# Attention in pairs of steps: one stretch of full-width matmuls, one of 32-column products

## The reference

```
x = x + attention(layernorm(x))
x = x + ffn(layernorm(x))          # base linear + top-2 of 8 rank-16 LoRA experts

attention: q, k, v = x@Wq.T, x@Wk.T, x@Wv.T    split into 16 heads of 32
           q, k = rope(q), rope(k)
           scores = q k^T / sqrt(32), causal mask
           ctx = softmax(scores) v;  out = ctx @ Wo.T
```

## Time and profile before

| | |
|---|---|
| median of 3 runs | 1838.37 us (1838.18 to 1847.95) |
| the profiled execution's own time, its span | 1836.8 us |
| PE busy | 1737.2 us, 95%, 9952 matmuls |
| DVE, POOL, ACT busy | 1167.2, 804.4, 784.3 us |
| granted TensorE clock, mean | 0.965 |

### The profile page before, as it was taken

The page is one execution under the profiler, slowest core; times in us unless marked ns, Lnnn a source line. Parts: engine busy times, 40 slices in busy tenths (PEclk is TensorE's granted clock), DMA queues, the critical chain, the costliest instruction groups (busy, mean ns, idle before and its releaser), DMA issues. The chain is left out here.

```text
span 1836.8 us, 33962 instructions
## 1 busy us (share of the span) xinstructions
PE 1737.2 (95%) x9952; PEld 1010.7 (55%) x9952; DVE 1167.2 (64%) x2630; ACT 784.3 (43%) x1544; POOL 804.4 (44%) x434
## 2 busy tenths in 40 slices
PE   6999995789999999989999998999999996999998
PEld 5888884444444444444445444444444433677776
DVE  6667663687767767657767775776776704566564
ACT  3222221135555545545555554554555563222321
POOL 1333333335655646535655564564664672111211
PEclk9999998599999989989999998999999997999999
DMA  5556545830161161142115006116102003131221
GB/s 172 201 197 220 194 166 174 185 72 24 25 139 25 25 131 33 25 90 70 30 35 124 25 10 137 25 25 135 29 25 71 12 7 101 41 134 69 83 100 47
DMA packets 103259, 157.60 MB, mean 86 GB/s; under 512 B 10544, under 2 KB 43824, under 8 KB 100400
## 3 DMA queue, kind: packets, MB, share of 16 engines
q1 hardware_dynamic: 93296, 136.10, 27.4%
q10 hardware_dynamic: 9792, 19.40, 2.9%
HBM read 96.23 MB, written 58.72 MB: 84 GB/s over the span
## 5 line engine op out<-in xcount | busy, mean ns | idle before, releaser
L771 ACT ACTIVATE a_probs<-a_st 128x512 f32<-128x512 f32 (+3 forms) x1280 | 613.2, 536 | 543.3 <-PE a_st L661 277.7
L618 POOL TENSOR_TENSOR a_pair<-a_probs 128x1024 f32<-128x1024 f32 (+2 forms) x320 | 614.8, 1938 | 396.7 <-ACT a_probs L771 396.7
L790 DVE TENSOR_REDUCE a_part<-a_mx 128x1 f32<-128x512 f32 x768 | 507.7, 684 | 208.8 <-PE a_mx L649 206.8
L649 PE MATMUL a_mx<-a_k_stack,a_q_stack 96*128 96x512 f32 (+3 forms) x1280 | 493.5, 428 | 45.1 <-DMA a_q_stack<-qk_scratch 24.5
L661 PE MATMUL a_st<-a_q_stack,a_k_stack 98*128 98x512 f32 (+3 forms) x1280 | 447.9, 393 | 5.1 <-ACT a_probs L771 2.2
L649 PEld LDWEIGHTS a_mx<-a_k_stack,a_q_stack 96*128 96x128 f32 x1280 | 229.7, 196 | 389.5 <-DVE a_part L790 179.5
L794 DVE CUSTOM_DVE_ANT_0 a_mx<-a_mx,a_mask 128x384 f32<-128x384 f32 (+3 forms) x512 | 250.5, 498 | 140.7 <-PE a_mx L649 138.1
L661 PEld LDWEIGHTS a_st<-a_q_stack,a_k_stack 98*128 98x128 f32 x1280 | 242.8, 193 | 83.6 <-ACT a_probs L771 52.7
L217 POOL TENSOR_TENSOR p_rot<-p_mul 128x1024 f32<-128x1024 f32 x32 | 90.7, 2836 | 213.3 <-DVE p_mul L412 213.3
L675 PE MATMUL a_av<-a_probs,shared 128*32 128x512 f32 (+3 forms) x1280 | 161.7, 551 | 0.7
L675 PE MATMUL a_av<-a_probs,a_v 128*32 128x512 f32 (+3 forms) x1280 | 160.0, 546 | 0.7
(11 more groups left out here) (138 smaller groups left out, 1656.8 us busy)
## 6 DMA issues: line engine op xcount, KB each, us to landing
a_q_stack<-qk_scratch SPq DMA_DIRECT2D x96, 256.0 KB, 4.9
a_k_stack<-qk_scratch SPq DMA_DIRECT2D x21, 1024.0 KB, 13.7
qk_scratch<-p_rot_hi SPq DMA_DIRECT2D x32, 512.0 KB, 3.1
qk_scratch<-p_rot_lo SPq DMA_DIRECT2D x32, 512.0 KB, 3.9
v_scratch<-p_v_st SPq DMA_DIRECT2D x32, 256.0 KB, 6.1
ctx_scratch<-a_ctx_st SPq DMA_DIRECT2D x32, 256.0 KB, 2.4
f_ctx<-ctx_scratch SPq DMA_DIRECT2D x8, 1024.0 KB, 8.9
f_x<-in_x SPq DMA_DIRECT2D x8, 1024.0 KB, 7.8
```

What stands on the lines that cost most here:

```text
L618: pool.tensor_tensor(pair[:, p % 2, h:h + 2, q0:TT], probs[:, s % RING, h:h + 2, q0:TT], probs[:, (s + 1) % RING, h:h + 2, q0:TT], ALU.add ...
L649: pe.matmul(mx_ps[k % BANKS][:, 0:width], q_stack[0:96, t, h, qi * P:(qi + 1) * P], k_stack[par][0:96, h, c * TT:c * TT + width], start=Tr ...
L771: act.activation(probs[:, s % RING, h, q0:TT], st_ps[:, (HG * s + h) % BANKS, q0:TT], ACT.Exp, scale=SCORE_SCALE).then_inc(exp_done, 1)
L790: dve.tensor_reduce(out, mx_ps[k % BANKS][:, :], AX.X, ALU.max).then_inc(max_done, 1)
```

## The change

LAG goes; the ring of probabilities has 4 steps, not 5. PE's `group` now goes by pairs. For pair p it first issues the eight scores of both steps of pair p+1, with the pair's items spread among them, and then `values_and_sums`: the values of both steps of pair p and then their sums, all 32-column products, in one stretch. The wait for the probabilities stands once before it, at the last head of the second step; the waits for the copied values, the turned sums and POOL's two adds stand inside. The semaphore `step_done` becomes `values_done`, one count per pair. ACT, DVE, POOL and SP loop over pairs as well. ACT may write pair p when pair p−2 is done, as POOL may. DVE turns a finished unit's sums at the beginning of the next pair, inverts them after that pair's first item and turns them back after its second. SP stores two pairs after the unit's end and loads queries at the end of the pair that issues a unit's last scores. `plan_items` spreads the same 160 items over 20 pairs (5 to 10 in each), and the first group takes up to 14 in a pair, where it took 7 in a step. The number of matmuls, exps, reductions, adds and DMAs stays.

```diff
-LAG = 2
-RING = 5
+RING = 4
+LAST_PAIR = [e // 2 for e in UNIT_END]
...
-PER_FIRST = 7
+PER_FIRST = 14
...
-    room = [width(s + 1) + width(s) + width(s - LAG) * ((s - LAG) % 2) + 1.0 for s in range(NSTEP)]
-    for e in UNIT_END:
-        room[(e + LAG) % NSTEP] -= 0.8
-        room[(e + LAG + 1) % NSTEP] -= 0.5
+    room = [width(2 * p + 2) + width(2 * p + 3) + 2 * width(2 * p) + width(2 * p + 1) + 0.5 for p in range(NPAIR)]
+    for e in LAST_PAIR:
+        room[(e + 1) % NPAIR] -= 1.0
...
+            def values_and_sums(g, par, p):
+                steps = (2 * p, 2 * p + 1)
+                t, j = STEPS[steps[0]]
+                unit_first, unit_last = j == 0, p in LAST_PAIR
+                q0, q1 = (max(0, STEPS[s][1] - t * SUB) * P for s in steps)
+                pe.wait_ge(exp_done, exps(g, steps[1], HG - 1))
+                if unit_first:
                     pe.wait_ge(av_copied, 4 * g + t + START)
+                for n, (s, q) in enumerate(zip(steps, (q0, q1))):
+                    for h in range(HG):
+                        mm = pe.matmul(av_ps[h * DK:(h + 1) * DK, q:TT], vb[par][:, j + n, h * DK:(h + 1) * DK],
+                                       probs[:, s % RING, h, q:TT], start=unit_first and n == 0,
+                                       stop=unit_last and n == 1, tile_position=(0, h * DK))
+                mm.then_inc(values_done, 1)
+                if unit_first:
+                    pe.wait_ge(sum_turned, 4 * g + t + START)
...
+                pe.wait_ge(pair_added, 2 * (NPAIR * g + p) + 2)
                 for h in range(HG):
...
             def group(g, par, use, next_use, first, last):
+                for p in range(NPAIR):
+                    items = [(n, k) for n, k in items_of_pair(p, first) if not (n and last)]
                     issued = 0
+                    for i in range(2 * HG):
+                        while issued < len(items) and issued * 2 * HG <= i * len(items):
                             n, k = items[issued]
                             item(g + n, (par + n) % 2, next_use if n else use, k)
                             issued += 1
+                        s, h = 2 * p + 2 + i // HG, i % HG
+                        if s < NSTEP:
+                            scores(g, par, s, h)
                         elif not last:
+                            scores(g + 1, 1 - par, s - NSTEP, h)
+                    for n, k in items[issued:]:
+                        item(g + n, (par + n) % 2, next_use if n else use, k)
+                    values_and_sums(g, par, p)
...
             def group(g, first):
+                for p in range(NPAIR):
+                    act.wait_ge(pair_done, pairs(g, p - 2))
+                    for s in (2 * p, 2 * p + 1):
...
             def group(g, first, last):
+                for p in range(NPAIR):
+                    items = [(n, k) for n, k in items_of_pair(p, first) if not (n and last)]
+                    ended = [(g - before, t) for before, t in unit_ended_before(p, 1) if not (before and first)]
+                    for unit in ended:
+                        turn_sums(*unit)
+                    for i, (n, k) in enumerate(items):
+                        item_max(g + n, k)
+                        for unit in ended:
+                            if i == 0:
+                                invert(*unit)
+                            if i == 1:
+                                turn_back(*unit)
...
+                    for n, t in units_ended_at_pair(p, first):
                         if not (n and last):
+                            issued = items_before(p + 1, first)
                             unit_max(g + n, t, NITEM * g + (min(issued, NITEM) if last else issued))
```

More of the change, by code:

```diff
@@ L619, in add_pairs @@
                                            probs[:, (s + 1) % RING, h:h + 2, q0:TT], ALU.add).then_inc(pair_added, 1)
-                    for ahead, t_out in unit_ended_before(s, 1):
-                        if not (ahead and first):
-                            divide(g - ahead, t_out)
+                    for before, t_out in unit_ended_before(p, 1):
+                        if not (before and first):
+                            divide(g - before, t_out)
             def divide(g, t):
@@ L680, in sums @@
[L680 to L699, removed]
+            def values_and_sums(g, par, p):
[5 more added lines that the diff above has]
+                if unit_first:
+                    pe.wait_ge(av_copied, 4 * g + t + START)
+                for n, (s, q) in enumerate(zip(steps, (q0, q1))):
[6 more added lines that the diff above has]
+                    pe.wait_ge(sum_turned, 4 * g + t + START)
+                if q1 > q0:
+                    for h in range(HG):
+                        pe.matmul(sum_ps[h * DK:(h + 1) * DK, q0:q1], ones[:, :], probs[:, steps[0] % RING, h, q0:q1],
+                                  start=unit_first, stop=False, tile_position=(0, h * DK))
+                pe.wait_ge(pair_added, 2 * (NPAIR * g + p) + 2)
+                for h in range(HG):
+                    mm = pe.matmul(sum_ps[h * DK:(h + 1) * DK, q1:TT], ones[:, :], pair[:, p % 2, h, q1:TT],
+                                   start=unit_first and q1 == q0, stop=unit_last, tile_position=(0, h * DK))
@@ L747, in _ @@
             pe.wait_ge(ones_done, 1)
-            for h in range(HG):
-                scores(0, 0, 0, h)
+            for s in range(2):
+                for h in range(HG):
+                    scores(0, 0, s, h)
             pe.wait_ge(first_values, 2 * 16)
@@ L858, in _ @@
             group(GROUPS - 1, False, True)
-            for part_of, _, _ in PARTS:
-                part_of(GROUPS - 1, QT - 1)
+            turn_sums(GROUPS - 1, QT - 1)
+            invert(GROUPS - 1, QT - 1)
+            turn_back(GROUPS - 1, QT - 1)
 class Early:
```

119 lines of the change are left out of this document (35 added, 84 removed).

## The result

The changed kernel takes 1867.33 us (median of 4, 1862.81 to 1876.22), the kernel before 1841.57 in the runs beside it: ratio 1.015, 95% interval 1.0112 to 1.0188. It is slower, as forecast. It lies 17 us above the forecast 1850, inside the stated range (1785 to 1890) and just outside the 1835 to 1865 that was given for the likeliest case. The loss is 26 us, where 12 were forecast. The profiled execution has a span of 1861.1 us at a mean granted clock of 0.94.

The account below looks back on a forecast made before the run. PE sets attention's pace. Per group 48.9 + 84.7 + 1.0 = 134.6, + 6.6 collision + 3.0 clock = 144.2 against 143.0; six times +7, first and last groups −1 + 3 + 1, unit rows +2: span 1849, runs 1850 us, range 1785 to 1890.

Parts of the forecast that it names:

- The collision: At units' maxima, DVE's CAST and subtraction wait for POOL's adds, delaying pairs 2, 12, 10 and 16: +6.6 us per group.
- The clock: Behind PE's waits in pairs 2 and 12, half clock for 3.4 us: 1.5 us each, +3.0 per group.
- Rival 3: Slow clock for long: 10 us at half speed behind each of 16 waits, 5 us each, 1905 us; chance 0.10.
- V: PE's stretch of 32-column products (values and sums) in each pair: 48.9 us per group, 2.81 at two full steps.
- F: PE's stretch of eight scores and n maxima in each pair, by the largest of three chains: 84.7 us per group.
- rival 1: No collision: POOL and DVE stay out of step at units' maxima, 134.6 us per group, 1783 in all; chance 0.24.
- One visit costs 0.28: Each PE visit to 32-column products costs 0.28 us beside its products; 60 become 20 per group, −11.3 us.
- 14.1 us of waits in place of 12.2: Per group, PE's waits for DVE and ACT after the change, against waits and exposed loads before it.
- the ends' −1 and +1: Outside the middle groups: first group −1 us; one step more of scores ahead at the start +1 us.
- 2: Rival: collision, but the clock stays; 141.2 us per group, about 1828 us in all; chance 0.16.
- 5: Rival: visits cost nothing when merged, the 0.28 reappears inside V; +11 us per group, about 1935 us; chance 0.02.
- Rival 4: Full stretches paced by DVE worse than the chain: 0.3 us more in each of 12 full pairs, 1875 us; chance 0.10.

Follow-up runs that it names:

- e1: Changed kernel with a unit's maximum on DVE done by four reductions instead of one reduction, a CAST and a subtraction: 1783.15 us, ratio 0.9675 to before.
- e4: Changed kernel with the third score of pairs 2 and 12 issued 15 times into its bank instead of once: 1843.63 us.
- e6: Kernel before with the unit's maximum by four reductions and DVE reading only 128 columns of each maximum's bank: 1824.0 us, ratio 0.9912.
- e5: Changed kernel with the unit's maximum by four reductions and DVE reading only 128 columns of each maximum's bank: 1705.74 us, ratio 0.9274.

## Why the prediction was right, and where it was not

*The collision: right, in place and mechanism.* It stands at all four units, as laid out: subtractions of 2.26 to 2.32 us for units 0, 1 and 2, a CAST of 1.41 for unit 3. The forecast time line for pairs 11 and 12 holds to some tenths: the CAST was to issue 1.2 us after the adds' start and did so after 1.56, and the subtraction was to end 4.7 after it (8.5 − 3.8) and ended after 4.72. Its size was off. Counted from the first full tile of a pair to that of the next, pair 2 takes 13.4 us and pair 12 12.8 (medians of groups 1 to 6, slow clock included), against 8.25 and 7.63 in e1: 5.2 each, where 2.5 and 2.6, with 1.5 of clock each, were forecast. Pair 10 lost 0.3 and pair 16 1.0, for 0.4 and 1.1. Per undisturbed group collision and clock together cost 147.5 − 136.0 = 11.5 us, against 6.6 + 3.0 = 9.6; with e4's price for the clock, the collision's part is 8.1 for 6.6.

*The clock: right in its price, with luck in its length.* 1.5 for each wait and 3.0 per group were forecast, and e4 gives 1.7 and 3.4. But the forecast reckoned 3.4 us at the lower level, and the windows above show 6.8. By the same reckoning (half of the stretch) that would have been 3.4 us for each wait; e4 puts it at half of this, and why so much of it costs nothing isn't shown. A direct view of the cost is the stretch of values and sums behind the wait of 611.97, which runs from 616.13 to 620.55, 4.42 us:

```profile
616.13 3.63 PE L672 MATMUL a_av<-a_probs,a_v 128*32 128x512 f32 x16
619.55 1.07 PE L684 MATMUL a_sum<-a_pair,a_ones 128*32 128x512 f32 x8
620.55 0.38 PE L643 MATMUL a_mx<-a_k_stack,a_q_stack 96*128 96x256 f32 x1
```

At the full clock the same products take 2.72 (below), so 1.7 us are lost here. Rival 3 (10 us at the lower level, 5 us for each wait) falls, its length less clearly than its price.

*The rest: near in its sum, wrong in its split.* Without collision the group was to take 134.6 and takes 136.0 (e1). That sum was built of V and F: V was put at 48.9 and takes 47.5, F at 84.7 + 1.0 and takes 88.5. The two misses have opposite signs and leave 1.4 us, which with the 1.9 of collision and clock makes the 3.3 between the forecast 144.2 and the 147.5. That rival 1's total of 1783 is e1's to the microsecond is luck.

The split of the way from 143.0 to it was further off. "One visit costs 0.28" fell short: 40 visits give 16.2 us (e6 less e5), not 11.3. And "14.1 us of waits in place of 12.2", with 1.0 added, priced the long stretch at 2.9 us where DVE's chain costs 9.3 (e1 less e5; in the old order the same edit gave 0.1). So one of the prediction's own signs of being wrong did show, "entries and exits that cost other than 0.28". By the table the two errors share a source, the 12.2 of before. They were taken for slack in whose place the new waits would come, but they were hardly waits: the table shows 0.9 of these, and exposed loads of 14.3. I had read the loads only behind visits, while they also stand where a maximum follows a maximum and where a score comes late.

*Single terms.* A full stretch of values and sums was 2.81 and is 2.72, as the start of the next maximum shows in the changed kernel's timeline (734.13 to 736.85):

```profile
734.13 1.92 PE L672 MATMUL a_av<-a_probs,shared 128*32 128x512 f32 x16
735.87 1.04 PE L684 MATMUL a_sum<-a_pair,a_ones 128*32 128x512 f32 x8
736.85 0.50 PE L643 MATMUL a_mx<-a_k_stack,a_q_stack 96*128 96x512 f32 x1
```

Counted to the end of the last values product of each part, the first six pairs lost 2.4 us (417.4 before, 419.8 after) and the rest of the first group 2.7, where the ends' −1 and +1 make 0 for both; the clock at the start of attention, low until 363.8 before and 373.9 after, may have a part in the first. The last group lost 2.9, for 3. Groups 1 to 6 lost 16.6, for 7 and the 2 allowed for unit 3's rows: most of the 12 us between the forecast span of 1849 and 1861 are here, and the undisturbed group alone was forecast at +1.2 and measured at +4.4.

*Rivals.* 1 is what the order would do without the collision (e1), 2 what it would do without the slow clock: it said 1828, and e4 brought 1843.6 with 210 added matmuls; the rest is the collision's part above. 5, that merged visits cost the same, is refuted by e5 and e6. Rival 4, full stretches of full tiles 0.3 worse than the chain, falls: the ten outside pairs 2 and 12 take 3.9 to 5.6 us, 4.87 in the mean, where 57.2 / 12 = 4.77 was forecast, and the 0.1 between them is pair 16's collision (4.78 in e1).

## What to carry to other kernels

When an order is changed, list the short DVE operations that read SBUF and ask what POOL will be doing when they issue: an operation of 0.175 us that meets an add of 2.36 costs not itself but everything queued behind it, and a form that does not collide can be had for nothing (84 us here). Merging visits to another tile shape pays (0.4 us each here) only as far as the other engines' banks outlast the longer stretch; spread the work that it holds up, or it comes back in a row. And read waits and exposed weight loads apart, from distances between starts, before calling either of them slack.

## What was not expected of the hardware

- A wait of 3.3 to 3.6 us on PE was followed by half clock, 6.8 us of it where the windows above look, and filling such waits with repeated matmuls made the kernel 24 us faster. Work that is thrown away paid for itself.
- Reductions from SBUF to SBUF (0.17 to 0.19 us), with rounding at the output as well, ran beside POOL's adds as fast as elsewhere, where a CAST and a subtraction of the same size stood for up to 1.5 and 2.3 us.
- Each visit to 32-column products less brought 0.40 us, where the rows at a visit's edges let expect 0.28.
